# Moving the causal-mask multiply of an attention kernel from VectorE to GpSimd

## The reference

```python
xn = _layernorm(x)
# attention: 16 heads of 64
q, k, v = split(einsum('bse,fe->bsf', xn, w_qkv))
scores = einsum('bhqd,bhkd->bhqk', q, k) / sqrt(64)
scores = where(tril(ones((S, S))), scores, -1e30)
out = einsum('bhqk,bhkd->bhqd', softmax(scores), v)
attn = einsum('bse,fe->bsf', out, w_out)
# experts: top-2 of 4 by xn @ wr + br, gates = softmax of the two logits
h = gelu(einsum('nd,edh->enh', xn, w1) + b1)        # exact gelu, hidden 4096
y = einsum('enh,ehd->end', h, w2) + b2
...
return x + attn + moe
```

## Time and profile before

| what | value |
|---|---|
| time before, median of 3 runs | 3256.48 us (3253.8 to 3257.7) |
| time of the profiled execution | 3253.77 us |
| its span (slowest core, 7) | 3252.2 us; the cores 3245.1 to 3252.2 us |
| attention, first scores to the expert block | 360.7 to 1251.6 us |
| PE, ACT, DVE, POOL busy over the span | 87%, 27%, 24%, 1% |
| mask multiplies L713 | 128 of 691 ns |
| exp L705 | 320 of 1113 ns |
| from the end of exp to a mask that finds DVE free | 0.11 us (550.74 + 1.11 to 551.96) |
| from one pair of `rrow` copies to the next | 12.85 us in qt 0, 20.89 us in qt 1 |
| clock granted to PE from 760 to 860 us | 0.50 |

### The profile page before, as it was taken

The page is one execution under the profiler, slowest core; times in us unless marked ns, Lnnn a source line. Parts: engine busy times, 40 slices in busy tenths (PEclk is TensorE's granted clock), DMA queues, the critical chain, the costliest instruction groups (busy, mean ns, idle before and its releaser), DMA issues. The chain is left out here.

```text
span 3252.2 us, 30076 instructions; the slowest of 8 cores (3245.1 to 3252.2 us)
## 1 busy us (share of the span) xinstructions
PE 2825.2 (87%) x11124; PEld 1082.1 (33%) x11124; DVE 785.1 (24%) x1057; ACT 863.8 (27%) x1169; POOL 36.3 (1%) x61
## 2 busy tenths in 40 slices
PE   3679667778878886999999999999999999999970
PEld 1234111111111113444444444444444444444420
DVE  4541443322212121111112111111111111111224
ACT  1212344545545541122211112211111221111100
POOL 0000000000000000000000000000000000000000
PEclk9789655565575558999999999999999999999955
DMA  6620100000000023033113303311330331230017
GB/s 150 91 46 1 26 7 20 1 26 1 0 26 13 13 29 75 1 52 52 23 30 52 52 1 52 52 20 33 52 52 1 52 52 17 35 52 1 1 57 253
DMA packets 79709, 127.86 MB, mean 39 GB/s; under 512 B 36174, under 2 KB 36302, under 8 KB 79314
## 3 DMA queue, kind: packets, MB, share of 16 engines
q0 software_dynamic: 33616, 75.50, 15.3%
q1 hardware_dynamic: 45954, 50.44, 5.1%
HBM read 176.26 MB, written 25.17 MB: 62 GB/s over the span
## 5 line engine op out<-in xcount | busy, mean ns | idle before, releaser
L868 PE MATMUL P<-xn_fm,w1g 128*128 128x512 bf16 x4096 | 896.5, 380 | 25.8 <-PEq L43 25.8
L899 PE MATMUL P<-w2g,h_sb 128*128 128x512 bf16 x4096 | 894.3, 379 | 0.0
L876 ACT ACTIVATE h_sb<-P,b_sb 128x512 bf16<-128x512 f32 x512 | 351.9, 687 | 1444.9 <-PE P L868 1444.9
L918 DVE SCALAR_TENSOR_TENSOR accum<-P,agate,accum 128x1024 f32<-128x1024 f32 x240 | 308.2, 1284 | 1379.8 <-PE P L899 1379.8
L868 PEld LDWEIGHTS P<-xn_fm,w1g 128*128 128x128 bf16 x4096 | 399.9, 98 | 513.9 <-issue 35.6
L899 PEld LDWEIGHTS P<-w2g,h_sb 128*128 128x128 bf16 x4096 | 400.8, 98 | 483.2
L705 ACT ACTIVATE p_sb<-P,cneg 128x1024 bf16<-128x1024 f32 x320 | 353.0, 1113 | 402.3 <-PE P L697 401.9
L726 PE MATMUL P<-p_sb,v_ext 128*65 128x512 bf16 x320 | 191.6, 599 | 123.2 <-DVE p_sb L713 65.7
L733 PE MATMUL P<-p_sb,v_ext 128*65 128x512 bf16 x320 | 194.7, 609 | 0.0
L713 DVE TENSOR_TENSOR p_sb<-p_sb,masks 128x1024 bf16<-128x1024 bf16 x128 | 88.0, 691 | 407.6 <-ACT p_sb L705 407.6
L697 PE MATMUL P<-q_fm,k_fm 64*128 64x512 bf16 x320 | 175.7, 608 | 0.0
(11 more groups left out here) (113 smaller groups left out, 942.2 us busy)
## 6 DMA issues: line engine op xcount, KB each, us to landing
w2g<-w POOLq DMA_DIRECT2D x16, 2048.0 KB, 28.8
w1g<-w POOLq DMA_DIRECT2D x15, 2048.0 KB, 18.2
attn_sc<-proj SPq DMA_DIRECT2D x16, 512.0 KB, 2.6
xrg<-x SPq DMA_DIRECT2D x4, 2048.0 KB, 10.6
arg<-attn_sc SPq DMA_DIRECT2D x4, 2048.0 KB, 15.5
y<-outr SPq DMA_DIRECT2D x16, 512.0 KB, 2.8
xA<-x SPq DMA_DIRECT2D x3, 2048.0 KB, 38.7
wqkv_bf<-w_qkv POOLq DMA_DIRECT2D x3, 2048.0 KB, 23.7
```

The lines of the kernel that those rows point to most:

```text
L868: t.matmul(PH67[par][:, 0:512], w1g[buf][:, dc * 1024 + hc * 128:dc * 1024 + (hc + 1) * 128], xn_fm[:, dc * 2048 + tt * 512:dc * 2048 + (t ...
L876: s.activation(h_sb[tt % 2][:, hc * 512:(hc + 1) * 512], PH67[par][:, 0:512], AF.Gelu, bias=b1_sb[:, e_ * 32 + g_ * 8 + hc:e_ * 32 + g_ * ...
L899: pt=pt, st=st, sp=sp: t.matmul(pt[:, half * 512:(half + 1) * 512], h_sb[tt % 2][:, hc * 512 + ts4 * 128:hc * 512 + (ts4 + 1) * 128], w2g[ ...
L918: v.scalar_tensor_tensor(accum[:, tsg * 1024:(tsg + 1) * 1024], pt[:, 0:1024], agate[:, tsg * 4 + e_:tsg * 4 + e_ + 1], accum[:, tsg * 102 ...
```

## The change

The multiply by the mask is issued by GpSimd. Its operands, its place in the order and its one use stay as they are. Its wait for the exp moves with it, and the AV matmuls wait for SG in place of SV.

```diff
         if p >= npair - 2:
             j = p - (npair - 2)
-            W("vector", "SS", ve)
-            vm = I("vector", "SV", lambda v, psb=psb, j=j: v.tensor_tensor(
+            W("gpsimd", "SS", ve)
+            vm = I("gpsimd", "SG", lambda g, psb=psb, j=j: g.tensor_tensor(
                 psb[:], psb[:], masks[:, j * 1024:(j + 1) * 1024], ALU.mult))
             v_use[p] = vm
-            v_uses[p] = "SV"
+            v_uses[p] = "SG"
```

## The result

The changed kernel takes 3352.64 us (median of 9 runs), the kernel before 3257.09 (10 runs); the ratio is 1.0295, 95% interval 1.0282 to 1.0309. The forecast was 3371 in a range of 3325 to 3415; against 3257.09 it was 114 us for a measured 96.

A forecast was written before the change was run, and what follows sets the result against it. PE paces unmasked attention; mask latency bounds masked steps. Added: 85.3 us for 23 head pairs, 19.3 for seven of qt 0, 3.7 for two projection pairs, 6.4 for late starts: 114.7 us, giving 3371, range 3325 to 3415.

The forecast's parts named there:

- PE waits for the mask's latency: Attention's masked steps: PE idles 65.7 us until a mask multiply ends; freeing DVE of 88.0 us buys little by itself.
- The chain A, B, D for M over 1.96: Tails of 23 head pairs: both heads' masks, then second head's next mask, in series; 3M + 3.51 us against 6.85.
- qt 0 by 2M - 1.95: Seven later head pairs of qt 0: two masks add time, less an earlier first start; 2M - 1.95 us each.
- M = 2.35 us: Duration of one mask multiply on GpSimd, taken as the middle of 1.91 and 2.78 us.
- two passes: GpSimd mask multiply reads its two inputs in turn: 1.91 us a mask.
- e = 0.1 us: Extra start delay of each waiting mask on GpSimd, between 0 and 0.44 us; adds 6.4 us in all.
- the first pair of qt 3: Head pair with a higher clock and less cover, priced the same as the other 22 of its kind.
- One pass: Rival: GpSimd takes two inputs at nearly the pace of one, 1.05 us a mask; 3274 us; chance 0.12.
- three passes: Rival: masks of 2.78 us on GpSimd with a late start of 0.44; 3430 us; chance 0.13.
- the packed pace: Rival: GpSimd handles packed bf16 pairs, 0.61 us a mask; 9 us less, 3248; chance 0.03.
- no effect: Rival: PE's queue hides masking anyway, or the multiply ends as early as now; 3256 us; chance 0.02.
- Contention: In qt 0, GpSimd's mask B and DVE's L668 and L676 wait for each other: at most 10 us.

The follow-up runs named there:

- the faster version: Kernel before plus scores ahead also across head pairs, slots copied out, narrow VectorE masks, Ln and Exp of sums a step earlier: 3116 us, ratio 0.9567.

## Why the prediction was right, point by point

- **PE waits for the mask's latency, and VectorE's 88 us of freed time are worth little.** Right. VectorE's busy time fell from 785.1 to 697.4 us and nothing came back from it but the earlier start of A in qt 0; three masks on VectorE (2.22 us) cost about what one on GpSimd does (2.115 us): 3.25% and 2.95%.
- **The chain A, B, D for M over 1.96.** Right: 9.86 us found, and 9.86 by the formula with the M found. The runs with half the masks show its parts singly (1.83 and 2.94 for 1.87 and 2.85 us).
- **qt 0 by 2M - 1.95.** Nearly: 2.43 us a pair for 2.28, or 2.36 with two late starts of 0.04.
- **M = 2.35 us.** The term that was mis-sized: 2.115 measured. The 87 us a microsecond make this 20 us of the sum. GpSimd's pace for two inputs, 1.89 ns an element, is 2.2 times that of its one-input rows (0.846), nearer to my two passes (1.91 us in all) than to three; the middle was too high. The estimate from the Trainium skill (GPSIMD Engine Reference, section 3.1) was 2.25 us, also above.
- **e = 0.1 us.** Measured 0.04 (0.15 against 0.11 behind exp's end). 4 us of the sum. The 0.44 us of a DMA issue says nothing of a multiply.
- **What lies outside the formula.** Left out were the clock in the first pairs of qt 2 and 3 (some 4 us over the formula), 1.8 us at the entry of the experts, and 3.1 us in the final sum. I tested none of these, and the cause of the last two stays open. I had priced the first pair of qt 3 like the others, though its cover is less; the trace shows it to be dearer, by 2.9 us. 108.3 + 6.4 = 114.7 us foreseen, 98.5 found in the profiled executions: 24 too much for M and e, 8 too little for the rest. The total is as near as this partly because the two errors have opposite signs.
- **Rivals.** One pass, three passes, the packed pace and no effect are out by the duration. Contention was put at 10 us at most and is nil in the changed kernel, where L668 and L676 last as long as before; the only contention found in any run had a VectorE instruction with two SBUF inputs, the mask itself.

## What to carry to other kernels

Ask of a small operation between two busy engines how long it is and what else the waiting engine has in its queue meanwhile, before asking which engine is free: here an engine at 1% load made the kernel 3% slower, and one reordered queue with a second buffer made a mask of the old length nearly free. Count the operations that share the new engine within one stretch: once they are longer than the spacing of their inputs (1.96 us here), one that had slack joins the chain. And when a wait is removed, look at once which wait is next: two of three steps towards the faster version lost time on their own, because the wait had only moved to ACT's queue.

## What the runs showed of the hardware

- A multiply of two bf16 tensors on GpSimd takes 2115 ns for 128x1024 and 1148 for 128x512; VectorE takes 691 and 423.
- A VectorE multiply with both inputs in SBUF that starts beside such a GpSimd instruction waits for it: 1.70 us for 0.69.
- VectorE's L668 and L676, with none and one of their inputs in SBUF, last 683 ns also where they lie wholly within a GpSimd mask.
- PE's clock in attention stayed at 0.50 in stretches in which PE was fed almost without a gap (the kernel before from 760 to 860 us, PE busy for 84.65 of the 100), and was higher in one window of 80 us of a run with shorter waits (0.60, PE busy for 58.53). What decides it, these runs don't settle.
